# Adjacency-masked attention block: scores and attention moved three units further ahead of the projections

## What is computed

```python
q, k, v = heads(x @ Wq + bq), heads(x @ Wk + bk), heads(x @ Wv + bv)
scores = einsum('bhqd,bhkd->bhqk', q, k) / sqrt(32)
scores = where(adj[:, None] == 0, -inf, scores)
out = einsum('bhqk,bhkd->bhqd', softmax(scores), v) @ Wo + bo
return layernorm(x + out)          # no gain or offset, eps 1e-5
```

## Time and profile before

| | us |
|---|---|
| median of 3 runs (lowest, highest) | 910.06 (909.27, 911.10) |
| the profiled execution | 910.95 |
| its span, first to last instruction | 909.2 |
| mean granted TensorE clock | 0.986 |
| PE busy | 870.0 (96%) |
| DVE busy | 809.6 (89%) |
| ACT busy | 689.1 (76%) |
| POOL busy | 273.0 (30%) |

### The profile page before, as it was taken

One profiled execution on the slowest core, in us unless ns is written; L12 is line 12 of the kernel. 1 busy time (PEld: TensorE's weight loads), 2 busy tenths in 40 slices (PEclk: granted clock), 3 DMA queues, 4 the chain that ended last, 5 costly groups with the idle time before them and its releaser, 6 DMA issues.

```text
span 909.2 us, 34909 instructions
## 1 busy us (share of the span) xinstructions
PE 870.0 (96%) x11784; PEld 606.9 (67%) x11784; DVE 809.6 (89%) x3449; ACT 689.1 (76%) x1745; POOL 273.0 (30%) x386
## 2 busy tenths in 40 slices
PE   6989999999999999999999999999999999999954
PEld 4666667777666777666777666777766677766632
DVE  5789899989899999999999999998989999999984
ACT  5787788777787887777877778877778788777761
POOL 0122233332323333323333223333232333322222
PEclk9999999999999999999999999999999999999967
DMA  8277887876678877678877677787667887667863
GB/s 301 60 148 135 140 175 172 179 160 151 129 166 179 176 161 148 149 143 176 179 167 169 125 151 168 172 178 167 142 137 159 179 177 161 149 148 149 149 140 93
DMA packets 362287, 143.33 MB, mean 158 GB/s; under 512 B 340752, under 2 KB 344848, under 8 KB 361872
## 3 DMA queue, kind: packets, MB, share of 16 engines
q1 hardware_dynamic: 362256, 142.93, 73.3%
HBM read 42.21 MB, written 16.78 MB: 65 GB/s over the span
## 4 chain that ended last, share of the span: by engine, by line
PE 71%; DVE 21%; issue 4%; DMA 2%; DVEq 1%; ACT 0%; SPq 0%; POOL 0%; POOLq 0%; ACTq 0%
PE proj_ps L610 57%; PE score_ps L610 7%; PE av_ps L610 6%; DVE masked L497 6%; DVE p_pair L484 5%; DVE stats L526 3%; DVE y L523 3%; DVE qT_lo L477 1%; DVE v_parts L470 1%; DMA pT<-p_pair 1%; DVE minus_max L497 1%; DVE inv_sum L506 1%; DMA w_land<-weights 1%; DVE attn L511 0%; DMA aT<-a_pair 0%
## 5 line engine op out<-in xcount | busy, mean ns | idle before, releaser
L412 ACT ACTIVATE probs<-masked,minus_max 128x128 f32<-128x128 f32 x1024 | 326.9, 391 | 170.3 <-DVE minus_max L497 165.9
L497 DVE CUSTOM_DVE_ANT_0 masked<-score_ps,mask 128x128 f32<-128x128 f32 x1024 | 236.9, 287 | 48.2 <-PE score_ps L610 29.8
L484 DVE SCALAR_TENSOR_TENSOR p_pair<-probs,p_pair 128x512 f16<-128x512 f32 x256 | 196.6, 768 | 1.3 <-ACT p_pair L422 1.1
L422 ACT ACTIVATE p_pair<-probs 128x512 f16<-128x512 f32 x256 | 161.3, 630 | 13.3
L610 PE MATMUL proj_ps<-wo_hi,aT 128*128 128x512 f16 x512 | 166.4, 387 | 2.4 <-DMA aT<-a_pair 1.5
L230 POOL TENSOR_TENSOR xT_lo<-xT_raw,xT_hi 128x512 f16<-128x512 f32 x60 | 70.0, 1166 | 309.3 <-ACT xT_hi L375 309.3
L610 PE MATMUL proj_ps<-xT_hi,wq_hi 128*128 128x256 f16 x512 | 141.3, 276 | 11.3 <-DVE wq_lo L578 7.9
L610 PE MATMUL proj_ps<-xT_hi,wk_hi 128*128 128x256 f16 x512 | 140.3, 274 | 2.6 <-DVE qT_lo L477 2.4
L610 PE MATMUL proj_ps<-xT_lo,wq_hi 128*128 128x256 f16 x512 | 140.7, 275 | 0.0
L610 PE MATMUL proj_ps<-xT_hi,wq_lo 128*128 128x256 f16 x512 | 140.7, 275 | 0.0
L610 PE MATMUL proj_ps<-xT_hi,wk_lo 128*128 128x256 f16 x512 | 139.7, 273 | 0.0
(11 more groups left out here) (58 smaller groups left out, 1523.0 us busy)
## 6 DMA issues: line engine op xcount, KB each, us to landing
xT_raw<-x_cols SPq DMA_DIRECT2D x32, 512.0 KB, 4.3
x_in<-x_rows SPq DMA_DIRECT2D x32, 512.0 KB, 5.0
out<-y SPq DMA_DIRECT2D x64, 256.0 KB, 2.6
adj_in<-adj SPq DMA_DIRECT2D x32, 128.0 KB, 2.4
pT<-p_pair SPq DMA_TRANSPOSE x256, 3.1
w_land<-weights SPq DMA_DIRECT2D x2, 1024.0 KB, 7.7
w_land<-weights SPq DMA_DIRECT2D x4, 256.0 KB, 5.5
x_res<-weights SPq DMA_DIRECT2D x1, 1024.0 KB, 9.6
```

The lines of the kernel that those rows point to most:

```text
L412: ins = act.activation(probs[s % 2][:, j * S:(j + 1) * S], masked[s % 2][:, j], ACT.Exp, bias=minus_max[s % 2][:, j:j + 1], scale=-1.0)
L422: act.activation(p_pair[s % NT][:, 0:HW], probs[s % 2][:], ACT.Copy, scale=P_UP).then_inc(p_hi_done, 1)
L484: dve.scalar_tensor_tensor(out=p_pair[s % NT][:, HW:2 * HW], in0=probs[s % 2][:], scalar=P_UP, in1=p_pair[s % NT][:, 0:HW], op0=ALU.mult, ...
L497: ins = dve.tensor_tensor_reduce(masked[s % 2][:, j], score_ps[j][:, s % HC], mask[par][:, s // KC], -EXP_SCALE, 3.0e38, ALU.add, ALU.min, ...
```

## The change

`AHEAD` = 4 takes the place of `LAG` = 3. In step s TensorE now runs `attend` of unit s and `scores` of unit s+4 (of the next group from step 4 on). The distance between the attention and the scores that stand side by side stays four units, but both stand three steps earlier against the banks. Group 0 makes up the difference by `FIRST`: scores of one unit in step 0 and of two units in each of steps 1 to 3. The two Y banks change places: graph 1 of the group before in step 5, graph 0 of the same group in step 7. What follows an attention moves with it on the other engines: `high_part_attn` and `low_part_attn` of graph 0 both to step 5, `make_mask` from step 5 to 3, the second `high_part_x` from step 5 to 4 and the second `low_part_x` from step 6 to 5.

```diff
-    TASKS = ((Q, 0), (Q, 1), (K, 0), (K, 1), (V, 0), (Y, 0), (V, 1), (Y, 1))
-    LAG = 3
+    TASKS = ((Q, 0), (Q, 1), (K, 0), (K, 1), (V, 0), (Y, 1), (V, 1), (Y, 0))
+    AHEAD = 4
+
+    FIRST = ((1,), (2, 3), (4, 5), (6, 7))
...
+    def scored(g, s, par):
+
+        if isinstance(g, int) and g == 0 and s < AHEAD:
+            return [(0, t, 0) for t in FIRST[s]]
+        if s < SLOTS - AHEAD:
+            return [(g, s + AHEAD, par)]
+        return [(g + 1, s + AHEAD - SLOTS, 1 - par)] if has_next(g) else []
+
+    def softmaxed(g, s, par):
+
+        if s > 0:
+            return scored(g, s - 1, par)
+        return [(0, 0, 0)] if isinstance(g, int) and g == 0 else [(g, AHEAD - 1, par)]
...
-                    if s in (2, 4) and at_least(g, 1):
-                        turn_attn(g - 1, s // 4)
-                    if s in (0, 2) and at_least(g, 2):
-                        store(g - 2, s // 2)
+                    if s == 1 and at_least(g, 2):
+                        store(g - 2, 1)
+                    if s == 2 and at_least(g, 1):
+                        turn_attn(g - 1, 1)
+                        store(g - 1, 0)
+                    if s == 5 and has_next(g):
+                        turn_attn(g, 0)
...
-                    if s in (3, 6) and has_x_next2(g):
-                        low_part_x(pool, g + 2, (s - 3) // 3, par)
+                    if s in (3, 5) and has_x_next2(g):
+                        low_part_x(pool, g + 2, (s - 3) // 2, par)
...
-                    if s in (0, 4) and at_least(g, 1):
-                        high_part_attn(g - 1, s // 4)
+                    if s == 1 and at_least(g, 1):
+                        high_part_attn(g - 1, 1)
+                    if s == 5:
+                        high_part_attn(g, 0)
...
+                        if i == 0:
+                            if s == 5:
+                                low_part_attn(g, 0)
+                            if s > 0 and TASKS[s - 1][0] != Y and has_next(g):
+                                low_part_bank(g + 1, *TASKS[s - 1], nxt)
+                            if s == 2 and at_least(g, 1):
+                                low_part_attn(g - 1, 1)
...
-                    if s == 5 and has_next(g):
+                    if s == 3 and has_next(g):
                         make_mask(g + 1, nxt, k + par)
...
+                    if not has_next(g):
+                        for unit_g, t, unit_par in scored(g, s, par):
+                            scores(unit_g, t, unit_par)
+                        attend(g, s, par)
+                        continue
+                    for unit_g, t, unit_par in scored(g, s, par):
+                        before, slot = back(unit_g, t, AHEAD)
+                        if exists(before):
+                            attend(before, slot, par)
+                        scores(unit_g, t, unit_par)
```

More of the change, by code:

```diff
@@ L275, in group @@
                 for s in range(SLOTS):
-                    before, slot = back(g, s, 1)
-                    if exists(before):
-                        turn_probs(before, slot)
+                    for unit_g, t, _ in softmaxed(g, s, par):
+                        before, slot = back(unit_g, t, 1)
+                        if exists(before):
+                            turn_probs(before, slot)
                     if s == 0 and has_next(g):
@@ L310, in _ @@
             turn_probs(LAST, SLOTS - 1)
-            store(LAST - 1, 0)
             turn_attn(LAST, 0)
@@ L345, in group @@
                 for s in range(SLOTS):
-                    if s == 1 and at_least(g, 2):
-                        normalize(g - 2, 1)
+                    if s == 1 and at_least(g, 1):
+                        normalize(g - 1, 0)
                     if s == 2:
@@ L353, in group @@
                         residual(g, 1, par, k)
-                    if s in (3, 6) and has_x_next2(g):
-                        low_part_x(pool, g + 2, (s - 3) // 3, par)
+                    if s in (3, 5) and has_x_next2(g):
+                        low_part_x(pool, g + 2, (s - 3) // 2, par)
                     if s == 7 and at_least(g, 1):
-                        normalize(g - 1, 0)
+                        normalize(g - 1, 1)
             pool.memset(minus_half[:], -0.5).then_inc(const_made, 1)
@@ L362, in _ @@
             all_groups(pool, group)
-            normalize(LAST - 1, 1)
             normalize(LAST, 0)
@@ L426, in group @@
                 for s in range(SLOTS):
-                    if s in (0, 4) and at_least(g, 1):
-                        high_part_attn(g - 1, s // 4)
+                    if s == 1 and at_least(g, 1):
+                        high_part_attn(g - 1, 1)
+                    if s == 5:
+                        high_part_attn(g, 0)
                     if s > 0 and TASKS[s - 1][0] != Y and has_next(g):
                         high_part_bank(g + 1, *TASKS[s - 1], nxt)
[L431 to L434, removed]
+                    for unit_g, t, _ in softmaxed(g, s, par):
+                        exponentials(unit_g, t)
+                        high_part_probs(unit_g, t)
+                    if s in (2, 4) and has_x_next2(g):
+                        high_part_x(g + 2, (s - 2) // 2, par)
             for h in range(2):
@@ L455, in _ @@
             all_groups(act, group)
-            high_part_attn(LAST, 0)
             high_part_attn(LAST, 1)
@@ L545, in group @@
                 for s in range(SLOTS):
[L546 to L559, removed]
+                    for i, (unit_g, t, unit_par) in enumerate(softmaxed(g, s, par)):
+                        masked_max(unit_g, t, unit_par)
+                        before, slot = back(unit_g, t, 1)
+                        if exists(before):
+                            low_part_probs(before, slot)
+                        if i == 0:
[6 more added lines that the diff above has]
+                        before, slot = back(unit_g, t, AHEAD)
+                        if exists(before):
+                            head_norm(before, slot)
+                    if s == 0 and at_least(g, 1):
                         y_and_moments(g - 1, 0, nxt)
+                    if s == 6 and at_least(g, 1) and has_next(g):
+                        y_and_moments(g - 1, 1, nxt)
                     if s == 1 and not at_least(g, 1):
@@ L662, in step_bank @@
                 if kind == Y:
-                    if not at_least(g, 1):
+                    of = g if i == 0 else g - 1
+                    if not exists(of) or not has_next(of):
                         return
-                    if i == 1:
-                        pe.wait_ge(y_summed, batch(g - 1, 0) + 1)
+                    if i == 0 and at_least(g, 1):
+                        pe.wait_ge(y_summed, batch(g - 1, 1) + 1)
                     elif has_next(g):
@@ L669, in step_bank @@
                     else:
-                        pe.wait_ge(y_summed, batch(g - 2, 1) + 1)
-                    y_bank(g - 1, i)
+                        pe.wait_ge(y_summed, batch(g - 1, 0) + 1)
+                    y_bank(of, i)
                     return
@@ L683, in step_bank @@
                     pe.wait_ge(split_out, split_no(g, V, 1) + 1)
-                elif at_least(g, 2):
-                    pe.wait_ge(y_summed, batch(g - 2, 1) + 1)
                 else:
-                    pe.wait_ge(split_out, split_no(g, K, 1) + 1)
+                    pe.wait_ge(y_summed, batch(g - 1, 0) + 1)
                 split_bank(g + 1, kind, i, nxt)
@@ L749, in _ @@
             all_groups(pe, group)
-            attend(LAST, SLOTS - 3, LAST % 2)
-            attend(LAST, SLOTS - 2, LAST % 2)
-            attend(LAST, SLOTS - 1, LAST % 2)
             y_bank(LAST, 0)
```

## The result

The changed kernel takes 972.11 us (median of 5 runs, 971.81 to 974.75), the kernel before 910.06 on the same chip: ratio 1.0685, 95% interval 1.067 to 1.070. I had forecast 919, in a range of 910 to 925. The sign was right and the size was wrong by 53 us.

A forecast was written before the change was run, and what follows sets the result against it. TensorE was taken to bound groups 1 to 30, so only its waits counted. 910.95 + 11.0 (steady state) + 7.7 (start) - 9.8 (end) = 919.9 us, or 919.0 against the median; range 910 to 925.

The forecast's parts named there:

- VectorE loses 0.57 us of issue at the turn: At the loop's jump back, VectorE's issue gap in the old trace; with a long step 0 it delayed the K bank.
- Steady waits of 0.5 a group: TensorE's waits in steps 6 and 7, for V's low part and graph 0's transpose: 14.5 us over groups 1 to 29.
- delay by `low_part_x`: In step 5, GpSimd's low_part_x overlaps VectorE's low_part_probs, which was to end 0.47 us late.
- M: Start of masked_max in step 5, the time from which the prediction counted the following steps.
- K bank's 0.25 given back: VectorE's 0.25 us lateness at the K bank after the turn, covered in 14 groups: -3.5 us.
- Group 30 costs about nothing: Group 30 has no low_part_x, so it was predicted to have almost no added wait.
- upper bound of the steady state: Groups 1 to 30 if low_part_probs runs its full 0.69 us after the GpSimd instruction: +15.4 us.
- Rival A: Graph 0's transpose stays hidden because low_part_x does not meet low_part_probs; steady state -2, whole 906 us; chance 0.13.
- M + 6.34 against M + 6.33: Without overlap, when TensorE could start step 7's Y bank after graph 0's transpose lands, against when it wanted to.
- The start: Group 0, with three more softmax units on VectorE and one more Y bank, was to lengthen: +7.7 us.
- The end: After group 30's last scores, fewer scores, attentions and Y banks remain: 36.2 us instead of 46.0, so -9.8 us.
- What it would show: Expected profile signs: aT and v_parts waits, K bank's wait gone, p_pair about 1.15 us, groups 1 to 30 some 820 us.

The follow-up runs named there:

- after_pad40: The changed kernel with 40 empty semaphore increments at the head of VectorE's queue, moving its loop from place 303 to 343: 927.4 us, ratio 1.016 to the kernel before.
- before_pad44: The kernel before with 44 empty increments at the head of VectorE's queue, so its loop begins at 303 instead of 259: 977.4 us, ratio 1.071.
- pad40_x67: after_pad40 with the second high_part_x moved to step 6 and the second low_part_x to step 7: 918.1 us, ratio 1.006 to the kernel before.

## Why the prediction was wrong

- **The failed step** is in the first part: "VectorE loses 0.57 us of issue at the turn". I took it for a fixed property of the loop, the same after. It holds only while VectorE's code of 293 instructions stays loaded, and the change moved the loop's start by 44 instructions to where it does not, at no cost in my sum. The gap became 3.5 us; after_pad40 and before_pad44 show it to be the place, worth 44 us here. No wait in the trace of before could show this; a body of 293 instructions and the number of those ahead of it could have made it a rival.
- **Steady waits of 0.5 a group**: right in place and in number, mis-sized by a third. They come to 0.35 to 0.4. The delay by `low_part_x` is 0.20, not 0.47, with 0.15 of a later M that I did not have. The K bank's 0.25 given back is as predicted: 54.45 us for two groups is +0.48, which I had at +0.75. Over the 13 turns after the first the windows have 6.5 us for some 9.8. "Group 30 costs about nothing" failed: it takes 27.6 us for 27.0, as graph 0's transpose lands after 3.9 us there. (By its own terms the upper bound of the steady state is +15.1, not +15.4.)
- **Rival A** (transpose hidden) did not come. pad40_x67 shows that it would not have, even with no `low_part_x` in the way: without it the wait per group is still 0.18. "M + 6.34 against M + 6.33" was right that nothing was left to cover a delay.
- **The start**, +7.7: it is +10.1. The V bank of step 6 began at 56.8, 0.9 us behind the walk when the 0.65 of a later first bank are taken off, and took 4.22 us instead of 2.7, most of it at 1.2 GHz. The walk had no clock in it.
- **Groups 1 to 3** were put down at the steady price. In after_pad40 they cost 9.5 us more than before, by late landings and the slow banks behind them. This is the second term that was missed. The same late landings are in the trace of before (4.4 to 6.8 us for five of the six transposes of groups 0 to 2), but the cover had been three steps, and TensorE did not wait.
- **The end**, -9.8: it is -9.3 in the windows of the changed kernel and -10.4 in after_pad40. This walk held, Y banks at the lower clock included.
- **Luck.** With the loop at a cheap place the new order costs 1.6%, so 925 us against 910.06, at the edge of the range of 910 to 925. That is no success of the sum: by the windows of after_pad40 it is 10.1 for the start, 9.5 for groups 1 to 3, 6.5 for the other turns, 0.6 for group 30 and 10.4 off at the end, where I had 7.7, steady waits alone, and 9.8. A steady wait that was too large hid part of the two terms that were missed.
- **What it would show**: the waits for aT and v_parts, and the K bank's wait gone, came as told; `p_pair` in step 5 is 0.89, not 1.15; groups 1 to 30 at 869 us and not 820 gave the miss away at once.

## What to carry to other kernels

When a hardware loop's body is longer than one block of instructions, as VectorE's 293 here, count the instructions ahead of it too: an edit that adds or removes code before the loop can change the price of every turn, in this kernel by 3 us and more, and a few empty instructions at a point where the engine waits anyway test and cure it. Compare two versions of such a kernel only with both loops at a cheap place; with both at the dear place the change would have looked like no loss at all (ratios to the kernel before of 1.0685 and 1.071, whose intervals overlap), where it costs 1.6% with both at a cheap one. And when a step is brought nearer to its user, price its slack for the worst case in the trace, not the steady one: here a landing of 4.6 instead of 3.1 us, followed by a bank mostly at half clock.

## What was not expected of the hardware

- The load of a loop's code costs VectorE 3.27 us per jump against 0.27, with five 8 KB packets in each turn. For a body of 293 the place turns dear between the 279th and the 291st instruction, and it is cheap again at the 343rd.
- Beside single waits of TensorE of 1.7 to 2.2 us the granted clock fell to 1.2 GHz for 3.4 or 6.8 us, within the wait or up to 1.3 us behind it, so that the wait cost 1.3 to 1.7 us more than itself, or 2.5 (banks of 4.08 and 5.30 for 2.73). It did so at all 13 jumps of before_pad44 and at 6 of the 13 of the changed kernel.
- In group 1 and the loop's first turn, graph 0's transposes beside a 16 KB instruction packet landed after 4.6 to 5.1 us for 3.1, with 7 to 15 GB/s moved in between (cause argued). A transpose beside an 8 KB packet took 3.85 us, and 3.05 where the padding had taken that packet away.
